# Sums of squares by a tile of ones in four column groups, turned by a block transpose on VectorE, in a gated delta rule kernel

## What is computed

```python
mixed = silu(causal_conv1d(xn @ w_qkv, conv_w))
q, k, v = split(mixed)
q = l2norm(q); k = l2norm(k)      # x * rsqrt(sum(x*x) + 1e-6)
core = gated_delta_rule(q * DK**-0.5, k, v, g, beta)
var = mean(core * core, axis=-1)
core = core * rsqrt(var + 1e-6) * norm_weight * silu(z)
out += core @ w_out
```

## Time and profile before

| | |
|---|---|
| time, median of 3 runs | 1450.18 us (1450.12 to 1452.05) |
| span of the profiled execution (first to last instruction) | 1450.2 us; no other time of it is given |
| TensorE matmul busy | 1303.2 us, 90% |
| VectorE busy | 1055.2 us, 73% |
| ScalarE busy | 706.5 us, 49% |
| GpSimd busy | 650.4 us, 45% |
| granted TensorE clock, mean | 0.958 |
| sums of the outputs, L1185, matmul records | 512 (x 247 ns, overlapping) |
| sums of the query, L1086, matmul records | 256 (x 245 ns, overlapping) |
| time, chain that ended last, by engine | TensorE 27%, VectorE 19%, GpSimd 11% |

### The profile page before, as it was taken

How to read it: one execution, slowest core, us unless ns; L and a number is a source line. 1 busy time by engine, 2 the same in 40 slices (tenths; PEclk the granted TensorE clock), 3 DMA queues, 4 the chain that set the end, 5 groups by cost and what they waited for, 6 DMA issues and landing times.

```text
span 1450.2 us, 29334 instructions
## 1 busy us (share of the span) xinstructions
PE 1303.2 (90%) x10040; PEld 1092.1 (75%) x10040; DVE 1055.2 (73%) x1948; ACT 706.5 (49%) x1241; POOL 650.4 (45%) x1041
## 2 busy tenths in 40 slices
PE   6789999999857989989899999989999899999958
PEld 4678888888635868778687887868778687787846
DVE  2975555555477798888979888897888888879424
ACT  3434333342226656556565655655655565565411
POOL 2122222221118366383754738366384654836430
PEclk9999999999979999999999999999999999999858
DMA  5111111100220303213030230303213031230101
GB/s 212 44 44 45 43 43 43 49 0 0 74 72 14 98 16 92 46 63 107 15 94 19 89 92 24 99 16 93 53 55 107 17 92 34 74 85 15 27 16 37
DMA packets 100815, 81.81 MB, mean 56 GB/s; under 512 B 86832, under 2 KB 89904, under 8 KB 97360
## 3 DMA queue, kind: packets, MB, share of 16 engines
q1 hardware_dynamic: 100688, 80.11, 18.5%
HBM read 68.36 MB, written 11.73 MB: 55 GB/s over the span
## 4 chain that ended last, share of the span: by engine, by line
PE 27%; DVE 19%; POOL 11%; issue 6%; DMA 4%; ACT 3%; SPq 1%; POOLq 0%; DVEq 0%; ACTq 0%
POOL halves L812 6%; DVE conv L944 5%; POOL halves L809 5%; DVE eg L955 4%; DVE nm L976 4%; PE rv L1194 4%; PE ra L1159 3%; PE pj L1055 3%; PE pj L1057 2%; PE pj L1056 2%; PE pk L1093 2%; PE ra L1141 2%; PE ra L1149 2%; DMA r_scratch<-halves 1%; PE rv L1167 1%
## 5 line engine op out<-in xcount | busy, mean ns | idle before, releaser
L944 DVE SCALAR_TENSOR_TENSOR conv<-pj,taps,conv 128x510 f32<-128x510 f32 (+2 forms) x384 | 284.6, 745 | 60.7 <-ACT conv L841 50.2
L812 POOL TENSOR_TENSOR halves<-halves 64x30 f32<-64x30 f32 (+14 forms) x480 | 262.6, 547 | 37.7
L809 POOL TENSOR_TENSOR halves<-halves 64x30 f32<-64x30 f32 (+14 forms) x480 | 249.2, 519 | 37.6
L1055 PE MATMUL pj<-xhi,whi 128*128 128x512 f32 x384 | 168.8, 440 | 14.9 <-DVE conv L944 13.0
L1194 PE MATMUL rv<-wo,gated 128*128 128x256 f32 x512 | 144.5, 410 | 31.7 <-DVE f L1019 30.0
L233 POOL TENSOR_TENSOR w1lo<-w,w1hi 128x2048 fp32r<-128x2048 f32 x10 | 46.0, 4604 | 256.5 <-ACT w2hi L253 256.5
L1057 PE MATMUL pj<-xhi,wlo 128*128 128x512 f32 x384 | 151.5, 394 | 0.0
L1056 PE MATMUL pj<-xlo,whi 128*128 128x512 f32 x384 | 150.6, 392 | 0.0
L955 DVE TENSOR_TENSOR_SCAN eg<-eg,start 128x384 f32<-128x384 f32 x128 | 135.8, 1101 | 13.6 <-issue 12.1
L803 POOL MEMSET halves<- 64x32 f32 x16 | 2.4, 150 | 314.4 <-DMA halves<-n_scratch 314.3
L976 DVE SCALAR_TENSOR_TENSOR nm<-pk,wneg,eg 128x512 f32<-128x512 f32 (+1 forms) x256 | 140.3, 611 | 3.4
(11 more groups left out here) (161 smaller groups left out, 3080.1 us busy)
## 6 DMA issues: line engine op xcount, KB each, us to landing
eg<-eg_scratch SPq DMA_DIRECT2D x16, 1536.0 KB, 7.7
wraw<-w_heads SPq DMA_DIRECT2D x16, 776.0 KB, 6.4
w<-w_up SPq DMA_DIRECT2D x10, 1024.0 KB, 4.8
n_scratch<-nm SPq DMA_DIRECT2D x64, 96.0 KB, 2.6
w<-w_down SPq DMA_DIRECT2D x10, 512.0 KB, 5.6
wo<-w_out SPq DMA_DIRECT2D x16, 256.0 KB, 4.9
halves<-n_scratch SPq DMA_DIRECT2D x32, 128.0 KB, 2.5
r_scratch<-halves SPq DMA_DIRECT2D x32, 128.0 KB
```

The costliest lines, as they stand in the source:

```text
L809: gp.tensor_tensor(tmp, rb[:, 0:t, t:t + 1].to_broadcast([4 * NM, t, w]), rb[:, t:t + 1, t + 1:].to_broadcast([4 * NM, t, w]), ALU.mult).t ...
L812: gp.tensor_tensor(rb[:, 0:t, t + 1:], rb[:, 0:t, t + 1:], tmp, ALU.add).then_inc(elim, 1)
L944: v.scalar_tensor_tensor(out=y, in0=pj[j % 2][:, :, 0:S - s], scalar=taps[par][:, piece(j)[0], KS - 1 - s:KS - s], in1=y, op0=ALU.mult, op ...
L1055: te.matmul(bank, whi[par][w], xhi[:, k, cols], start=(k == 0), stop=False)
```

## The change

The column of ones becomes a tile of 128x32 ones. It is now the stationary operand, and the squares are the moving one. For SO there are four products, one for each group of 32 columns of the array; group c takes the tokens c to c+31 of each of the 16 slices of 128 tokens (512 columns) and writes its sums to the 32 partitions c to c+31 of the bank, every one of these 32 rows being the same. SQ does so with 256 columns. VectorE then transposes the bank in blocks of 32x32 into a part of `sq` that is free at that time, after which the sum of a token stands on its own partition, in each column of a block. `sqe` reads the first column of every block from SBUF, `f2` too, now in two instructions, one for each value head, each after a wait for the transpose. SA is gone, and SO does all 16 slices. ScalarE's squares of the query now wait until VectorE has emptied SO's bank, and those of O0 until it has emptied SQ's.

```diff
--- before.py
+++ after.py
@@ -81,7 +81,7 @@
         xlo = sb("xlo", [P, KD, T], F32R)
         start = sb("start", [P, EC])
         ident = start[:, 0:P]
-        ones = sb("ones", [P, 1])
+        ones = sb("ones", [P, C32])
         beta = sb("beta", [P, HK, NT, REP])
         coef = sb("coef", [P, EA, NT])
         nwneg = sb("nwneg", [P, 1])
@@ -562,6 +562,8 @@
             tc2 = sb("tc2", [P, NM, C32], F32, c3)
             p1 = sb("p1", [P, NM, C32], F32, c3)
             f2 = sb("f2", [P, NT, REP], F32, c3)
+            qsum = sq[:, 0, :].rearrange("p (t x) -> p t x", x=C32)
+            osum = sq[:, 0:2, :].rearrange("p m (t x) -> p (m t) x", x=C32)
             fr = sb("fr", [P, NT, REP], F32, c3)
             pj = [c3.enter_context(nc.psum_tensor(f"pj{i}", [P, 2, S], F32)) for i in range(2)]
             pk1 = c3.enter_context(nc.psum_tensor("pk1", [P, 2, S], F32))
@@ -594,6 +596,8 @@
             v_free = sem("rv_emptied", c3)
             o_sq = sem("output_squared", c3)
             f_step = sem("norm_factor_step", c3)
+            q_turned = sem("query_sums_turned", c3)
+            o_turned = sem("output_sums_turned", c3)
             f_root = sem("norm_factor_root", c3)
             acc_step = sem("acc_first_head", c3)
             init = sem("heads_init", c3)
@@ -603,7 +607,7 @@
 
 
 
-            ORDER = ("K0 P4 P5 SA TR0 K1 SO P6 OUT0 OUT1 K2 TR1 TR2 TR3 P7 OUT2 P8 OUT3 P9 P10 OUT4 P11 LA1 K3 LA2 P0 P1 "
+            ORDER = ("K0 P4 P5 TR0 K1 SO P6 OUT0 OUT1 K2 TR1 TR2 TR3 P7 OUT2 P8 OUT3 P9 P10 OUT4 P11 LA1 K3 LA2 P0 P1 "
                      "LB1_0 LB1_1 LB2_0 LB2_1 OUT5 U1_0 OUT6 U1_1 OUT7 SQ N21_0 N21_1 U2_0 U2_1 P2 O0 VT0 O1 P3 VT1 O2 O3 "
                      "VT2 VT3").split()
             ORDER_A = ("P4 P5 TR0 S4 P6 W SO TR1 TR2 S5 P7 P8 TR3 P9 SQ S6 P10 LA1 P11 LA2 P0 LB1_0 LB1_1 S7 LB2_0 LB2_1 P1 "
@@ -618,7 +622,7 @@
 
             EARLY = {"W", "P0", "P1", "P2", "P3", "S0", "S1", "S2", "S3"}
             FRONT = {"P", "S", "SQ", "SK", "K", "VT"}
-            TAIL = {"SA", "SO", "OUT"}
+            TAIL = {"SO", "OUT"}
             VTAIL = RING_V["SO"] + RING_V["OUT"]
             AFIRST, VFIRST = RING_A["VT"], RING_V["SQ"]
             APER, VPER = sum(RING_A.values()), sum(RING_V.values())
@@ -877,7 +881,7 @@
                         elif item == "SQ":
                             a.wait_ge(silu_made, 8 * n + 4)
                             if "SO" in it.vpos:
-                                a.wait_ge(v_full, it.v("SO"))
+                                a.wait_ge(v_free, it.v("SO"))
                             a.activation(sq[:, 0:B, :], kq[:, :, 1, :], ACT.Square).then_inc(sq_made, 1)
                         elif item == "SK":
                             a.wait_ge(small, 16 * n + 14)
@@ -923,6 +927,8 @@
                             ins.then_inc(a_free, 1)
                         elif k == "O":
                             i = number(item)
+                            if i == 0 and "SQ" in it.vpos:
+                                a.wait_ge(v_free, it.v("SQ"))
                             a.wait_ge(v_full, it.v(item))
                             a.activation(sq[:, 2 * i:2 * i + 2, :], it.vbank[item][:].rearrange("p (r s) -> p r s", r=2),
                                          ACT.Square).then_inc(o_sq, 1)
@@ -988,8 +994,10 @@
                             convolve(*group(it, number(item)), number(item))
                         elif item == "SQ":
                             v.wait_ge(v_full, it.v(item))
-                            v.tensor_scalar(sqe[par][:], it.vbank[item][:, 0:NT], EPS_L2, EPS_RMS * P,
-                                            ALU.add, ALU.mult).then_inc(v_free, 1)
+                            v.transpose(qsum, it.vbank[item][:, 0:NT * C32].rearrange("p (t x) -> p t x", x=C32)
+                                        ).then_inc(q_turned, 1)
+                            v.wait_ge(q_turned, n + 1)
+                            v.tensor_scalar(sqe[par][:], qsum[:, :, 0], EPS_L2, EPS_RMS * P, ALU.add, ALU.mult).then_inc(v_free, 1)
                         elif k == "K":
                             decays(n, par, number(item))
                         elif item == "LA1":
@@ -1016,9 +1024,14 @@
                                                    op0=ALU.mult, op1=ALU.mult).then_inc(v_free, 1)
                         elif item == "SO":
                             v.wait_ge(v_full, it.v(item))
-                            v.scalar_tensor_tensor(out=f2[:], in0=it.vbank[item][:, 0:NT * REP].rearrange("p (t r) -> p t r", r=REP),
-                                                   scalar=1.0 / P, in1=sqe[par][:].unsqueeze(2).to_broadcast([P, NT, REP]),
-                                                   op0=ALU.mult, op1=ALU.add).then_inc(v_free, 1)
+                            v.transpose(osum, it.vbank[item][:].rearrange("p (t x) -> p t x", x=C32)).then_inc(o_turned, 1)
+                            v.wait_ge(o_turned, b)
+                            for r in range(REP):
+                                ins = v.scalar_tensor_tensor(out=f2[:, :, r].rearrange("p (i c) -> p i c", c=2),
+                                                             in0=osum[:, :, 0].rearrange("p (i r c) -> p i r c", r=REP, c=2)[:, :, r, :],
+                                                             scalar=1.0 / P, in1=sqe[par][:].rearrange("p (i c) -> p i c", c=2),
+                                                             op0=ALU.mult, op1=ALU.add)
+                            ins.then_inc(v_free, 1)
                         elif k == "OUT":
                             t = number(item)
                             if t == 0:
@@ -1082,9 +1095,10 @@
                         elif item == "SQ":
                             bank = fill_v(it, item)
                             te.wait_ge(sq_made, n + 1)
-                            for t in range(NT):
-                                ins = te.matmul(bank[:, t:t + 1], sq[:, t // 2, t % 2 * P:t % 2 * P + P], ones[:],
-                                                start=True, stop=True)
+                            for c in range(0, P, C32):
+                                ins = te.matmul(bank[c:c + C32, 0:NT * C32], ones[:],
+                                                sq[:, 0:B, :].rearrange("p b (t x) -> p (b t) x", x=P)[:, :, c:c + C32],
+                                                start=True, stop=True, tile_position=(0, c))
                             ins.then_inc(v_full, 1)
                         elif k == "K":
                             i = number(item)
@@ -1176,16 +1190,14 @@
                                 ins = te.matmul(bank[:, r * S + P:(r + 1) * S], zz[:, BH + s, :], nm[odd][:, s, 1, S:EC],
                                                 start=False, stop=True)
                             ins.then_inc(v_full, 1)
-                        elif item in ("SA", "SO"):
-
-                            te.wait_ge(o_sq, 4 * (b - 1) + (2 if item == "SA" else 4))
-                            bank = fill_v(it, "SO") if item == "SA" else it.vbank[item]
-                            for t in range(0, NT // 2) if item == "SA" else range(NT // 2, NT):
-                                for r in range(REP):
-                                    ins = te.matmul(bank[:, t * REP + r:t * REP + r + 1], sq[:, t // 2 * 2 + r, t % 2 * P:t % 2 * P + P],
-                                                    ones[:], start=True, stop=True)
-                            if item == "SO":
-                                ins.then_inc(v_full, 1)
+                        elif item == "SO":
+                            te.wait_ge(o_sq, 4 * (b - 1) + 4)
+                            bank = fill_v(it, item)
+                            for c in range(0, P, C32):
+                                ins = te.matmul(bank[c:c + C32, :], ones[:],
+                                                sq[:].rearrange("p m (t x) -> p (m t) x", x=P)[:, :, c:c + C32],
+                                                start=True, stop=True, tile_position=(0, c))
+                            ins.then_inc(v_full, 1)
                         elif k == "OUT":
                             t = number(item)
                             te.wait_ge(wo_in, 16 * (b - 1) + 16)
```

## The result

The changed kernel takes 1462.07 us in the median of five runs (1455.4 to 1464.7); the kernel before, measured beside it, 1450.18 (1446.7 to 1456.5). The ratio is 1.0066, with a 95% interval of 1.0041 to 1.0091: slower by 0.4 to 0.9%, or about 9.6 us (the two medians, of five runs each that scatter by some 10 us, lie 11.9 us apart). The forecast was 1457.3 us, slower, within 1449 to 1467. The profiled execution has a span of 1462.6 us.

What follows compares the result with a forecast made beforehand. VectorE's circuit was taken to bound the kernel, with TensorE pacing the first stretch. On 1450.2 us: 14 x (0.83 - 0.42) = +5.7, clock +3.4, end -2.0, giving 1457.3 us; range 1449 to 1467.

Steps and rivals of the forecast that it cites:

- The circuit: First stretch at TensorE's pace, K0 to f2 at VectorE's, then both through OUT1 and K2; 61.5 us a group.
- GpSimd's path: GpSimd and DMAs bringing the inverse blocks: 61.0 us a group, so a faster kernel could gain 0.5 us a group.
- SO on VectorE, 0.83 us more: SO's PSUM transpose (0.75 us) and second f2 (0.08) add 0.83 us a group, all on the path.
- (c): Rival: SO's transpose out of PSUM makes the cost 1.58 us instead of 0.83, giving 1468 us; chance 0.12.
- SA and SO on TensorE, worth nothing: TensorE saves 2.5 us a group, worth nothing because it waits for VectorE before K1 and OUT1.
- rival (b): Column groups take turns: between 1445 and 1462 us, about 1456 with four low-clock stretches gone; chance 0.15.
- SQ, 0.42 us a group: In the first stretch, SQ's shorter products let N21_0 start 0.42 us earlier a group, on the path.
- The clock, +3.4 us: Longer stalls before OUT1 lower TensorE's clock behind them in two of four more groups, 1.7 us each.
- rival (a): Low-clock stretch moves to the wait before K1, hidden in slack, saving 1.7 us a group spared: 1445.4 us; chance 0.12.
- The end, -2.0 us: After the last squares, shorter TensorE work lets the last f2 and OUT0 come sooner: 2.0 us gained.
- The sum: Whole kernel: 1450.2 us with +5.7, clock +3.4 and end -2.0 gives 1457.3 us, slower.

Runs made afterwards that it cites:

- the filled stall: The changed kernel with OUT0's two products issued four times, filling TensorE's wait before OUT1: 1452.6 us, ratio 0.9999 to the kernel before.

## Why the prediction was right

- **The circuit**. Right. The transpose twice and not at all show that VectorE's work in SO counts, about with its full length, and the filled stall shows that 2.6 us more of TensorE's work beside it cost nothing. The 61.5 us that I took for a group includes the short group 14 (57.9); the fourteen steady ones take 61.7, so the distance to GpSimd's path of 61.0 us was 0.7 us and not 0.5. That path was read in one group and is no floor: with the stall filled, several groups take 60.1 to 60.9 us.
- **SO on VectorE, 0.83 us more.** Measured 0.90 more (0.98 in place of 0.08): the transpose out of PSUM took 0.70 us for 512 columns, 0.05 less than taken, the wait behind it 0.04, and the two f2 together 0.24 where twice 0.08 stood. The rival of a dear transpose (c) is out. The Trainium skill (VectorE: DVE Perf Modes, The three transpose paths) led to an estimate of 1.24 us; the measured 0.70 decides.
- **SA and SO on TensorE, worth nothing.** Right, with the stalls as given: 2.17 us before K1 (forecast 1.9) and 4.0 before OUT1 (4.2). The column groups work side by side, so rival (b) is out. The Trainium skill (TensorEngine Tiling (Array Packing), PSUM Bottleneck) warns that tiling speeds up TensorE but not the reading of PSUM. The trace agrees: for all 16 slices the products went from 2 x 1.70 to 1.06 us and their reading from 0.08 to 0.98 us.
- **SQ, 0.42 us a group.** The first stretch went from 29.86 to 29.43 us, which is the 0.42; the kernel with SO alone puts SQ at 0.37 us, within wide limits. Alone, in the kernel before, it bought nothing that can be told, and the prediction did not say that its worth depends on the rest of the change.
- **The clock, +3.4 us.** This is the term that was mis-sized, in the number of groups and not in the price. I took two groups of four, on the ground that the new wait before K1 might draw the low stretch to itself. In the profiled execution of the changed kernel it never did: all fourteen groups are low after OUT1. The four that were at 1.00 grew by 8.8 us in all; less 0.45 each for the other terms leaves 7.0, or 1.75 each where the price was 1.7, and that is the upper end that I had set. The mechanism of rival (a) is real, and it stood in the kernel before already: in two of the four groups (6 and 8) the low stretch lay at K1, which the prediction had as "begun elsewhere" without saying where. It showed again in three groups with SO alone and in seven with the stall filled. The lower end of rival (b) rests on a misreading: a stall of 2.14 us did not as such keep full clock, for stalls of 2.09 and 2.15 us (groups 3 and 4) were followed by a low one. What decides between two stalls of one length was not found. Two of four was thus a guess, and the time came inside the range because the range had been drawn to hold all four.
- **The end, -2.0 us.** Measured -3.0 (50.35 to 47.33). After the last squares f2 was ready 1.5 us earlier, where 1.9 was computed, and another 1.2 us came from what I had left out: the additions of OUT0 waited 1.20 us for TensorE before, and now not at all.
- **The sum.** 4.5 + 8.8 - 0.1 - 3.0 = 10.2 us, to which the profiled execution adds the 2.2 us of the unchanged front: 1450.2 + 12.4 = 1462.6. The ratio of the runs, 9.6 us, agrees with the 10.2. The forecast had 7.1: SO and SQ came out 0.6 us dearer in all, the clock 3.6 dearer, and the end gained 1.0 more than forecast, which took a part of it back.

## What to carry to other kernels

Ask which engine a saving is handed to. A faster reduction on TensorE that leaves a wider result in PSUM moves work to the engine that reads it, and here that engine had no idle time in just this stretch: price each part in the stretch where it lies, since the same edit gained 0.4 us a group in one place and lost 0.9 in the other. A stall that gets longer on an engine off the path was not free here, for in four more groups the clock fell behind it, at 1.75 us each: look at what the engine must do right behind the stall, and who waits for that. And before giving a chance to where a low stretch will lie, look up where it lies in every group of the kernel at hand.

## What the runs showed that was not expected

- TensorE's clock fell with hardly any idle time (0.43 us) behind a run of one-column products, in the kernel before with OUT0 three times. It was low after 2.6 us of such products and 1.39 us of idle time in the stall; with 2.6 us of 256-column products in the same place and 1.1 to 1.5 us of idle time it stayed full. The busy share on the page was 90% before and 86% after, at mean clocks of 0.958 and 0.957: it tells neither.
- More work made the changed kernel faster: three more copies of OUT0, 9.7 us less (uncertain by 5 us). With SO ahead of K1, work added in the same way gained nothing.
- The same stall was followed by a low clock in one group and not in another: 2.1 us in the kernel before, and 2.8 us in the kernel without SO's transpose.
- Waits of TensorE at LA1 of 2 to 3.5 us, which mean that it was early, were followed in several groups of the experiments by a low clock in the part that it paces; the longest such groups take 65.0 us (SQ alone), 66.0 (SO ahead of K1 in the kernel before) and 66.6 (SO ahead of K1 and OUT1 four times). So the gain of an earlier TensorE can be lost in the same group.
